# Two more units of lead for the turned rows of a routed expert stage, paid for with output buffers

## The reference, cut to what matters

```
gelu = lambda t: jax.nn.gelu(t, approximate=False)
shared = gelu(x @ W1s + b1s) @ W2s + b2s
rw = jax.nn.softmax(x @ Wr, axis=-1)
topw, topi = jax.lax.top_k(rw, K)                       # K = 2, E = 8
topw = topw / jnp.sum(topw, axis=-1, keepdims=True)
...
h = gelu(jnp.einsum('bsd,edf->bsef', x, W1p) + b1p)      # D = 128, F = 512
priv = jnp.einsum('bsef,efd->bsed', h, W2p) + b2p
routed = jnp.einsum('bsed,bse->bsd', priv, mask)
return shared + routed
```

## Time and profile before

| | us |
|---|---|
| median of 3 runs | 1564.83 (1561.16 to 1564.96) |
| the profiled execution's own time | 1566.65 |
| its span | 1564.8 |
| PE busy | 1238.3 (79%) |
| DVE busy | 1101.2 (70%) |
| ACT busy | 984.6 (63%) |
| POOL busy | 876.4 (56%) |
| PE, mean granted clock over the span | 0.939 |

### The profile page before, as it was taken

The page is one execution under the profiler, slowest core; times in us unless marked ns, Lnnn a source line. Parts: engine busy times, 40 slices in busy tenths (PEclk is TensorE's granted clock), DMA queues, the critical chain, the costliest instruction groups (busy, mean ns, idle before and its releaser), DMA issues. The chain is left out here.

```text
span 1564.8 us, 33624 instructions
## 1 busy us (share of the span) xinstructions
PE 1238.3 (79%) x9505; PEld 706.7 (45%) x9506; DVE 1101.2 (70%) x2467; ACT 984.6 (63%) x1713; POOL 876.4 (56%) x922
## 2 busy tenths in 40 slices
PE   2999999999999999837899977888888888878300
PEld 1566666666666666623344433333443333334100
DVE  3688898888899888845677764555565555555288
ACT  1677777777777777625677766676776767667200
POOL 3246666666666666536756652556565656555500
PEclk9999999999999999968899998999999999999755
DMA  2012222122222211122354322333233333333099
GB/s 59 28 55 64 68 67 65 62 65 63 65 67 67 66 62 47 42 68 75 109 147 126 115 62 51 72 65 79 67 74 67 75 69 77 67 67 80 10 333 312
DMA packets 225698, 128.33 MB, mean 82 GB/s; under 512 B 128175, under 2 KB 203998, under 8 KB 225644
## 3 DMA queue, kind: packets, MB, share of 16 engines
q1 hardware_dynamic: 191596, 85.44, 21.6%
q0 software_dynamic: 17408, 33.87, 6.4%
q10 hardware_dynamic: 16640, 8.39, 1.8%
HBM read 47.37 MB, written 55.09 MB: 65 GB/s over the span
## 5 line engine op out<-in xcount | busy, mean ns | idle before, releaser
L935 DVE SCALAR_TENSOR_TENSOR h<-hid,h 128x512 f16<-128x512 f32 x416 | 286.1, 693 | 265.6 <-ACT h L915 223.3
L1224 POOL DMA_INDIRECT pairs_dram<-x_rows x288 | 294.1, 1021 | 104.1 <-issue 104.0
L915 ACT ACTIVATE h<-hid 128x512 f16<-128x512 f32 x416 | 261.9, 630 | 57.8 <-remote 10.6
L887 PE MATMUL Y<-h,w 128*128 128x512 f16 x1248 | 292.0, 384 | 7.1 <-DVE h L935 4.4
L876 PE MATMUL Z<-x_rows,w 128*128 128x512 f16 x864 | 209.8, 395 | 93.0 <-issue 76.3
L926 ACT ACTIVATE hid<-Z,biases 128x512 f32<-128x512 f32 x416 | 279.8, 673 | 0.0
L887 PEld LDWEIGHTS Y<-h,w 128*128 (+1 forms) x1248 | 122.5, 99 | 163.9 <-issue 22.3
L419 DVE TENSOR_REDUCE smax<-S 128x8 f32<-128x1024 f32 x128 | 155.8, 1217 | 47.4 <-PE S L642 47.4
L1029 POOL DMA_INDIRECT slots_dram<-x_rows,pair_slot x140 | 143.4, 1024 | 70.5 <-issue 40.6
L876 PEld LDWEIGHTS Z<-x_rows,w 128*128 x864 | 81.8, 101 | 201.0 <-issue 121.5
L422 DVE TENSOR_TENSOR probs<-S,smax 128x1024 f32<-128x1024 f32 x128 | 156.8, 1225 | 16.1 <-DVE smax L419 3.4
(11 more groups left out here) (165 smaller groups left out, 2092.5 us busy)
## 6 DMA issues: line engine op xcount, KB each, us to landing
y_pairs<-pairs_dram SPq DMA_DIRECT2D x32, 512.0 KB, 6.0
x_res<-in_x_dram SPq DMA_DIRECT2D x32, 256.0 KB, 3.2
adj<-in_adj_dram SPq DMA_DIRECT2D x32, 256.0 KB, 3.0
x_rows<-x SPq DMA_DIRECT2D x32, 256.0 KB
xT_dram<-xT SPq DMA_DIRECT2D x32, 256.0 KB
xTu<-xT_dram SPq DMA_DIRECT2D x32, 256.0 KB
out_dram<-x_res ACTq DMA_DIRECT2D x16, 512.0 KB, 10.1
pairs_dram<-x_rows POOLq DMA_INDIRECT x288
```

The costliest lines, as they stand in the source:

```text
L887: mm = pe.matmul(self.Yt[:, b], self.w2[:, m, :, c][:, e, :], self.h16[:, b, k, c], start=c == 0 and n == 0, stop=c == FC - 1 and n == 2)
L915: act.activation(self.h16[:, b, 0, c], self.hid[:, c], ACT.Copy, scale=HS).then_inc(self.hi_done, 1)
L935: dve.scalar_tensor_tensor(out=self.h16[:, b, 1, c], in0=self.hid[:, c], scalar=HS, in1=self.h16[:, b, 0, c], op0=ALU.mult, op1=ALU.subtra ...
L1224: pool.indirect_dma_start(pairs_dram, bass.IndirectOffsetOnAxis(ap=pair_of[n][:, j:j + 1], axis=0), y_sb[n % NIN][:, j], None, bounds_chec ...
```

## The change

Three numbers part ways that were one. Buffers of turned rows become 8 (NIN), of which a load may run ahead by 6 (LEAD): the rows of unit u are asked for once `keep_y(u - 6)` is done. The output buffers `y_sb` become 2 (NY) instead of 4, so `keep_y(u)` waits for the send of unit u - 2 to have landed, not of unit u - 4. The buffers of pair numbers stay 8, with one semaphore each as before; the `turned` semaphores become 8 and the `sent` semaphores 2. No instruction of any engine's work is added or removed.

```
--- before.py
+++ after.py
@@ -1169,34 +1169,35 @@
     f.semaphores(nc, ctx, "r")
 
     spare = x_rows[:, :, :].rearrange("p t c -> p (t c)")
-    NIN = 4
-    NID = 8
+    NY = 2
+    NIN = 8
+    LEAD = 6
     f.xT = spare[:, 0:NIN * 2 * UT].rearrange("p (n a t) -> p n a t", n=NIN, a=2)
     at = NIN * 2 * UT
     y_sb = [spare[:, at + n * 2 * UT:at + (n + 1) * 2 * UT].bitcast(F32).rearrange("p (j c) -> p j c", c=P)
-            for n in range(NIN)]
-    at += NIN * 2 * UT
-    pair_of = [spare[:, at + n * 2 * GT:at + (n + 1) * 2 * GT].bitcast(U32) for n in range(NID)]
+            for n in range(NY)]
+    at += NY * 2 * UT
+    pair_of = [spare[:, at + n * 2 * GT:at + (n + 1) * 2 * GT].bitcast(U32) for n in range(NIN)]
     slot_halves = slots_dram.bitcast(F16)
     turned = [sem(f"rows_turned{n}") for n in range(NIN)]
-    numbers_in = [sem(f"numbers_in{n}") for n in range(NID)]
-    sent = [sem(f"y_sent{n}") for n in range(NIN)]
+    numbers_in = [sem(f"numbers_in{n}") for n in range(NIN)]
+    sent = [sem(f"y_sent{n}") for n in range(NY)]
     block = ctx.enter_context(nc.Block())
     U = NU
 
     def octets(eng, unit):
 
-        for u in range(NID):
+        for u in range(NIN):
             unit(u, u)
-        with eng.Fori(1, U // NID - 1) as r:
-            for n in range(NID):
-                unit(NID * r + n, n)
-        for n in range(NID):
-            unit(U - NID + n, n)
-
-    def turns(u, n):
-
-        return (u - n) * (16 // NIN)
+        with eng.Fori(1, U // NIN - 1) as r:
+            for n in range(NIN):
+                unit(NIN * r + n, n)
+        for n in range(NIN):
+            unit(U - NIN + n, n)
+
+    def turns(u, n, buffers):
+
+        return (u - n) * (16 // buffers)
 
     def early(u, n=0):
         return isinstance(u, int) and u < n
@@ -1204,10 +1205,10 @@
     @block.sync
     def _(sp):
         def load(u, n):
-            if not early(u, NIN):
-                sp.wait_ge(f.back_read, u + 1 - NIN)
+            if not early(u, LEAD):
+                sp.wait_ge(f.back_read, u + 1 - LEAD)
             row = sp.value_load(unit_start[0:1, bass.ds(u, 1)], min_val=0, max_val=BLANK)
-            sp.dma_start_transpose(f.xT[:, n % NIN], slot_halves[bass.ds(row, UT), 0:2 * P]).then_inc(turned[n % NIN], 16)
+            sp.dma_start_transpose(f.xT[:, n], slot_halves[bass.ds(row, UT), 0:2 * P]).then_inc(turned[n], 16)
             sp.dma_start(pair_of[n].unsqueeze(2), slots_dram[bass.ds(row, UT), P:P + 1].rearrange("(j p) o -> p j o", p=P),
                          allow_slow_non_contiguous=True)\
                 .then_inc(numbers_in[n], 16)
@@ -1218,18 +1219,18 @@
     def _(pool):
         def send(u, n):
             pool.wait_ge(f.back_read, u + 1)
-            pool.wait_ge(numbers_in[n], (u - n) * (16 // NID) + 16)
+            pool.wait_ge(numbers_in[n], turns(u, n, NIN) + 16)
             f.take_wait(pool, u)
             for j in range(GT):
                 pool.indirect_dma_start(
                     pairs_dram,
                     bass.IndirectOffsetOnAxis(ap=pair_of[n][:, j:j + 1], axis=0),
-                    y_sb[n % NIN][:, j], None,
-                    bounds_check=TOP * NT * P - 1, oob_is_err=False).then_inc(sent[n % NIN], 16)
+                    y_sb[n % NY][:, j], None,
+                    bounds_check=TOP * NT * P - 1, oob_is_err=False).then_inc(sent[n % NY], 16)
 
         octets(pool, send)
-        for n in range(NIN):
-            pool.wait_ge(sent[n], 16 * GT * U // NIN)
+        for n in range(NY):
+            pool.wait_ge(sent[n], 16 * GT * U // NY)
 
     @block.tensor
     def _(pe):
@@ -1237,8 +1238,8 @@
             return pe.value_load(unit_expert[0:1, bass.ds(u, 1)], min_val=0, max_val=E - 1)
 
         def unit(u, n):
-            pe.wait_ge(turned[n % NIN], turns(u, n % NIN) + 16)
-            f.hidden(pe, u, expert(u), n % NIN)
+            pe.wait_ge(turned[n], turns(u, n, NIN) + 16)
+            f.hidden(pe, u, expert(u), n)
             if not early(u, 1):
                 f.output(pe, u - 1, expert(u - 1), 1 - n % 2)
             if not early(u, 2):
@@ -1261,8 +1262,8 @@
     def _(dve):
         def keep_y(u, n):
             dve.wait_ge(f.back_ps, u + 1)
-            if not early(u, NIN):
-                dve.wait_ge(sent[n], turns(u, n) * GT)
+            if not early(u, NY):
+                dve.wait_ge(sent[n], turns(u, n, NY) * GT)
             dve.tensor_copy(y_sb[n], f.B7[:, :].rearrange("p (j c) -> p j c", j=GT)).then_inc(f.back_read, 1)
 
         def keep_yT(u, b):
@@ -1274,12 +1275,12 @@
             if not early(u, 1):
                 keep_yT(u - 1, 1 - n % 2)
             if not early(u, 2):
-                keep_y(u - 2, (n - 2) % NIN)
+                keep_y(u - 2, n % NY)
 
         octets(dve, unit)
-        keep_y(U - 2, NIN - 2)
+        keep_y(U - 2, 0)
         keep_yT(U - 1, 1)
-        keep_y(U - 1, NIN - 1)
+        keep_y(U - 1, 1)
 
 
 def combine_phase(nc, ctx, x_res, pair_weight, pairs_dram, out):
```

## The result

The changed kernel took 1554.05 us (median of 6 runs, 1550.05 to 1563.51); beside it on the same chip the kernel before took 1565.32 (6 runs, 1561.16 to 1568.07). The ratio is 0.9941, interval 0.9919 to 0.9964: 0.6% faster, where 6% were forecast, and 38 us above the upper end of the range. The profiled execution took 1559.72 us, with a span of 1557.9.

What follows compares the result with a forecast made beforehand. The prediction took PE's wait for late turned rows as the routed stage's bound, with PE itself next at 5.62 us a unit. Its sum, -3.0 - 104.3 + 15 = -92.3 us, gave 1472.5 us, range 1455 to 1512.

Steps and rivals of the forecast that it cites:

- The wait for rows goes: Routed stage: with lead 6 PE no longer waits before Z for turned rows; idle there falls from 93 to under 15 us.
- 3.0 + 104.3: Routed stage: Z(4) starts 3.0 us earlier, and the 67 units after it take 104.3 us less, at 5.62 us each.
- The stalls: Routed stage: units not running at the floor add 15 us, chosen between 5 and 49.
- Stalls as in the shared stage: Rival, routed stage: units take 6.35 us as in the later shared stage, gain 58.6 us, time 1506; chance 0.15.
- Two output buffers cost nothing: DVE's keep_y, waiting for the send two units back: cost zero, 7.9 us needed against 11.24 for two units.
- GpSimd slowed by DVE: Rival, sends: DVE lengthens indirect DMAs until POOL bounds; 1491 us with two of four slowed, 1552 with all; chance 0.07.
- The landing of sends binds: Rival, output buffers: late landings make two units take 14.60 us, 7.30 each, slower at 1570 us; chance 0.03.
- the wait is not for rows: Rival, before Z: the 4.2 to 4.6 us follow any load, so earlier loads move nothing, 1562 to 1565 us; chance 0.03.
- the 1.48: Landing of a send: 1.48 us assumed, from a POOL copy that waited for row scatters of 128 rows.
- the 8.21: Landing of a send: upper end of 8.21 us, from the last indirect DMA's end to SP's first read of the next stage.
- The clock inside the 5.62: Routed stage, PE: the faster clock from shorter gaps is already within the 5.62 us a unit, not an added gain.
- The end: After the last units: the tail runs as now, 0 us added, chosen between 0 and 3.

Runs made afterwards that it cites:

- before_again: The unaltered kernel before, run once more for its profile on chip 6, one of the undisturbed chips: 1537.98 us in one run.
- after_again: The changed kernel, unaltered, on chip 6, an undisturbed chip, against the kernel before there: 1440.16 us, ratio 0.9378.
- the first pair: The changed kernel and the kernel before, side by side on the chip of the result: 1554.05 and 1565.32 us.
- after: The trace of the changed kernel on the chip of the result; its profiled execution took 1559.72 us.
- before: The kernel before the change; its trace is the one the prediction was made from, profiled execution 1566.65 us.
- lead4_y2: The changed kernel with the lead set back to four units, leaving two output and eight input buffers, against the kernel before: 1535.28 us, ratio 0.9994.
- lead6_y4_again: The changed kernel with four output buffers kept instead of two, on chip 6, against the kernel before: 1440.64 us, ratio 0.9383.
- the two kernels with artificial holds: Changed kernel and kernel before, each with extra matmuls holding PE in 26 units: 1509.56 and 1571.57 us with 13 matmuls, 1593.13 and 1642.31 with 23.
- plain_sends: The changed kernel with its four indirect DMAs a unit replaced by plain DMAs to consecutive rows, chip 4, against the kernel before: 1452.05 us, ratio 0.9279.

## Why the prediction was wrong, point by point

- **The wait for rows goes: right.** It is gone in every trace with lead six. On an undisturbed chip the unit is 5.62 us as forecast, and the routed stage is 99.4 us shorter. The forecast of 3.0 + 104.3 was made from units of 7.18 us, measured on a chip that holds increments back; with the 7.05 of before_again ((502.8 - 2.4) / 71, where 2.4 us lie between the first and the last Z matmul of a unit) it would have been 3.0 + 67 x 1.43 = 98.8. One reading was wrong on the way, without harm: "done about 9.2 us after Z(u - 6)". The rows show `keep_y(20)` done 9.19 us after Z(22), so `keep_y(u - 6)` is done 9.2 us after Z(u - 4), and the wait goes with 4 x 5.62 - 14.6 = 7.9 us to spare, not 19. The forecast that each load is issued some 20 us before its Z misses for this reason: it is 12.7 us in the median of after_again, and 4 x 5.62 - 9.2 - 0.8 = 12.5 by the right count.
- **The stalls: the step that failed.** "I choose 15 us, nearer the low end", between 5 and 49. On the first chip the term was 107.3 - 9.5 = 98 us by the two traces of the first pair (508.3 to 498.8): from Z(4) to Z(71) it took 474.2 us, where the sum had 376.5 + 15. It was 95 by the same kernel on two chips. On an undisturbed chip it is about 2 us (378.9 against 376.5). The sign that the prediction named for this, idle time before Y and before ACT's first instruction with no releaser, is what the profile shows. What the prediction took for the low end, that the routed stage showed few "remote" waits, was true, and no measure of what was to come. GpSimd paused in most units then. Its waits in the trace of before, 942 to 1478 us:

```profile
POOL turn_pool L866 <- DVE x_rows L1266: 124.4, 58, 34.0
```

  Without the first, of 34.0 us, that is 57 pauses of 1.6 us. That they let held increments go before much waited for them is my reading. It fits that in this trace three or more came at once 10 times, and only once more than three; in after it was 24 times, and 22 times more than three. (40 of the 250 increments have no record in before, so some may be missing from this count.)
- **"Stalls as in the shared stage", the rival at 0.15,** had the right mechanism and too small a price: 7.0 us a unit instead of 6.35. That stage's 3.27 us at once looks like the same thing: just before it ACT had stood for 2.89 us with no releaser named. What the prediction lacks is that this cost grows as the stage gets faster, from 5.5 to 95 us. My explanation, which no run tests by itself: faster units take GpSimd's pauses away, so a hold lasts over a whole send; ACT and DVE run dry, with them GpSimd, and then the hold ends. That feedback brings the stage back almost to its old pace. The wait for rows, too, covered part of what holds the kernel before had; it takes in 1.7 us of each artificial one.
- **Two output buffers cost nothing: right.** lead4_y2 is 0.9994 of before; after_again and lead6_y4_again differ by 0.5 us. DVE did wait for landings, 11 times and 21.4 us in after_again, late in the stage when GpSimd had fallen behind. That is the sign which the prediction named for being wrong in the landing, but PE did not feel it.
- **GpSimd slowed by DVE: small.** The mean indirect DMA is 1.067 us in after_again against 1.023 in before_again; the pace stayed PE's.
- **The landing of sends binds, and the wait is not for rows: both excluded** by the same runs. For landings there are rows now, from DVE's waits in after_again:

```profile
1268.25 0.97 POOL L1225 DMA_INDIRECT pairs_dram<-x_rows  x1 [0.30 <-issue]
...
1270.51 0.69 DVE L1267 COPY x_rows<-B 128x512 f32<-128x512 f32 x1 [1.22 <-DMA pairs_dram<-x_rows]
```

  The copy could begin 1.29 us after the last DMA of that send had ended, and in DVE's twelve waits of the whole stage it was 1.2 to 3.0 us: the 1.48 was right, and the 8.21 far off. A send was late there not by its landing but because GpSimd had begun it late.
- **The clock inside the 5.62: right where nothing stalls** (1.00 in after_again from 942 to 1340 us), and not on the first chip, where it fell to 0.94.
- **The end: nearly right.** 0 was chosen between 0 and 3 us. From the last start of Z to the end of the span it is 111.4 us against 109.4 on the first chip, 110.2 against 109.1 on the other.
- **Luck on the good chips.** There the change gains 94.4 us, and 92.3 were forecast. That is two errors which cancel: the wait for rows was worth less than was reckoned, and the stalls cost almost nothing.

Shown, on the chips that do it: the late increments of the routed stage come with the indirect sends, and not with PE's pace, its table reads or the turned loads. Shown on the others: the change itself is worth 6.2%. That it takes indirect DMAs close together, and that a pause of GpSimd ends a hold, rests on the attention stage, on the times of release and on the two kernels with artificial holds, not on a run that changes the pauses alone.

Open: what it is in the indirect DMAs that does it. Plain sends differ from them in three things: GpSimd spends 545 ns instead of 1020 on each, it has longer pauses between sends (216.5 us of waits), and their rows lie together. The longer pauses between sends don't explain it alone, as the four DMAs of a plain send are closer together than the indirect ones. A kernel with indirect sends and pauses put in by hand, or one with indirect sends to rows that lie together, on a chip of the first kind, would tell more; neither was tried. Plain sends had two runs, on one chip.

Open as well is what differs between the chips, and one rival that no run here excludes. In the disturbed traces records of increments are missing, of the landings of the sends most of them (1310 of 4608 are there in after, 4402 in after_again, all in plain_sends). Every run on record has a span and a granted clock beside its time, so there is none that was surely free of recording. Whether the holds belong to the kernel alone, or come only while increments are being recorded on such a chip, was not tested.

## What to carry to other kernels

Before a stage is made faster, look at what its disturbances cost now and what covers them: a wait on "remote" or an unexplained gap of 3 us in a neighbouring stage with the same engines is worth more than the small total of such waits in a stage that still has slack, and its price may grow as the slack goes (here from 5.5 to 95 us). Compare the moment of a semaphore's increment with the work that it reports; an engine that idles although its input has long been made is not slow, it has been told late. And where a large change moves little, time the same two kernels on another chip before taking the change apart.

## What the runs showed of the hardware that was not expected

- On the chips of the result, 11 and 4 (the first may be one of the two others) TensorE's semaphore increments came up to 6 us and more after the matmuls, up to six at a time within 0.3 us; on chips 8, 6 and 9 some 95% and more came 0.3 to 0.4 us after the start of the last matmul. The kernel before takes 1564 to 1565 us on the ones and 1535 to 1537 on the others; the changed one 1554 (and 1452 with plain sends) against 1440 to 1441.
- On those chips the holds occur where GpSimd issues indirect DMAs one close behind the other. In the attention stage 28 of 33 increments were late beside a second DMA begun 1.3 to 1.4 us after the first, and 1 of 130 beside single ones (after). Trains of four, in the routed stage, held for up to 6 us and more; the increments came 1.7 to 2.8 us after the last of the four began. With plain DMAs in the same queue 319 of 319 were on time.
- Increments of ScalarE, VectorE and GpSimd were never recorded late, in the same trace in which half of TensorE's recorded ones were (121 of 235; after, 1000 to 1300 us).
- A plain DMA issue by GpSimd took 545 ns where an indirect one took 1020 to 1067.
- An indirect send of 128 rows of 512 bytes had landed 1.2 to 3.0 us after GpSimd's instruction ended (after_again, twelve waits).
- Matmuls of 128x512 start 0.216 us apart though each is recorded with 0.379.
